# Attention scores contracted over 128 rows, and two memory regions placed alike by 512 bytes

## What is computed

```python
mod = silu(c) @ ada_w.T + ada_b            # shifts, scales, gates
h   = modulate(rmsnorm(x), scale_msa, shift_msa)
q, k, v = split(h @ qkv_w.T + qkv_b)       # 16 heads of 36
q, k = rmsnorm(q) * 36 ** -0.5, rmsnorm(k)
o   = softmax(q @ k.T) @ v
x   = x + tanh(gate_msa) * (o @ proj_w.T + proj_b)
h2  = modulate(rmsnorm(x), scale_mlp, shift_mlp)
x   = x + tanh(gate_mlp) * (gelu(h2 @ fc1_w.T + fc1_b) @ fc2_w.T + fc2_b)
```

## Time and profile before

| what | us |
|---|---|
| median of 3 runs (lowest to highest) | 2906.13 (2906.03 to 2906.17) |
| the profiled execution | 2906.52 |
| its span in the trace | 2904.7 |
| first stage, to 436 us | 436 |
| attention, 436 to 1867 us | 1431 |
| PE busy in the span | 2880.2 (99%) |
| DVE / ACT / POOL busy | 1968.6 / 1578.1 / 213.3 |

### The profile page before, as it was taken

One profiled execution on the slowest core, in us unless ns is written; L12 is line 12 of the kernel. 1 busy time (PEld: TensorE's weight loads), 2 busy tenths in 40 slices (PEclk: granted clock), 3 DMA queues, 4 the chain that ended last, 5 costly groups with the idle time before them and its releaser, 6 DMA issues.

```text
span 2904.7 us, 35301 instructions
## 1 busy us (share of the span) xinstructions
PE 2880.2 (99%) x12990; PEld 2175.9 (75%) x12990; DVE 1968.6 (68%) x2727; ACT 1578.1 (54%) x1924; POOL 213.3 (7%) x161
## 2 busy tenths in 40 slices
PE   8999999999999999999999999999999999999999
PEld 7999986666666666666666666788888888888887
DVE  7777778899888888888888887844344243424342
ACT  4334336776776677677677666634344343434342
POOL 1323310101000000000000000090000000000000
PEclk9999999999999999999999999999999999999999
DMA  6555554221322322222222223432222222322121
GB/s 229 164 190 171 176 172 131 87 77 59 88 74 77 85 76 63 81 80 78 76 80 68 74 84 92 137 122 86 74 86 74 82 78 87 98 90 87 41 69 50
DMA packets 238454, 282.67 MB, mean 97 GB/s; under 512 B 34960, under 2 KB 144016, under 8 KB 237392
## 3 DMA queue, kind: packets, MB, share of 16 engines
q1 hardware_dynamic: 233408, 270.80, 30.4%
q10 hardware_dynamic: 4880, 9.70, 1.0%
HBM read 195.50 MB, written 84.67 MB: 96 GB/s over the span
## 4 chain that ended last, share of the span: by engine, by line
PE 94%; DVE 3%; ACT 1%; DMA 1%; issue 0%; SPq 0%; POOL 0%; POOLq 0%; DVEq 0%; ACTq 0%
PE ps L1645 16%; PE ps L1670 16%; PE ps L1733 15%; PE ps L1715 15%; PE ps L1657 13%; PE ps L794 12%; PE ps L1691 4%; PE ps L1656 2%; PE ps L749 1%; ACT gated L1314 1%; DMA gain<-kg 0%; DVE p_lo L1457 0%; DVE x L1517 0%; PE ps L741 0%; DVE w_lo L1510 0%
## 5 line engine op out<-in xcount | busy, mean ns | idle before, releaser
L1258 ACT ACTIVATE p_r<-ps 128x1024 f32<-128x1024 f32 x512 | 491.8, 1025 | 406.4 <-PE ps L1645 406.4
L1457 DVE TENSOR_TENSOR p_lo<-p_r,p_hi 128x1024 fp32r<-128x1024 f32 x512 | 613.7, 1220 | 0.0
L1645 PE MATMUL ps<-qT,kT 110*128 110x512 f32 x2048 | 574.7, 398 | 2.8 <-DMA kT<-qk_hi_scratch 1.7
L1645 PEld LDWEIGHTS ps<-qT,kT 110*128 110x128 f32 x2048 | 382.8, 190 | 137.7 <-issue 51.4
L1258 ACT ACTIVATE prob<-ps 128x1024 f32<-128x1024 f32 x512 | 483.5, 1031 | 3.1 <-PE ps L1645 2.8
L1656 PE MATMUL ps<-prob,vp 128*64 128x512 f32 x1024 | 453.1, 595 | 0.0
L1657 PE MATMUL ps<-prob,vp 128*37 128x512 f32 x1024 | 451.7, 594 | 0.0
L1587 DVE TENSOR_TENSOR a_lo<-act,a_hi 128x512 fp32r<-128x512 f32 x144 | 101.6, 706 | 508.2 <-ACT a_hi L1301 508.2
L1451 DVE CAST p_hi<-p_r 128x1024 fp32r<-128x1024 f32 x512 | 350.5, 695 | 135.7 <-ACT p_r L1258 134.2
L1733 PE MATMUL ps<-a_hi,w 128*128 128x512 f32 x1296 | 415.4, 393 | 0.0
L1670 PE MATMUL ps<-p_hi,vx 128*128 128x512 f32 x1024 | 404.3, 395 | 0.1
(11 more groups left out here) (194 smaller groups left out, 3556.0 us busy)
## 6 DMA issues: line engine op xcount, KB each, us to landing
w_raw<-w SPq DMA_DIRECT2D x144, 320.0 KB, 2.9
qk_hi_scratch<-aw SPq DMA_DIRECT2D x32, 576.0 KB, 3.2
qk_lo_scratch<-aw SPq DMA_DIRECT2D x32, 576.0 KB, 4.4
kT<-qk_hi_scratch SPq DMA_DIRECT2D x128, 144.0 KB
qT<-qk_hi_scratch SPq DMA_DIRECT2D x128, 144.0 KB
v_scratch<-stv SPq DMA_DIRECT2D x32, 512.0 KB, 2.7
vp<-v_scratch SPq DMA_DIRECT2D x16, 1024.0 KB, 9.2
xb<-xT SPq DMA_DIRECT2D x8, 1280.0 KB, 10.9
```

Of the source, the lines that this page charges most:

```text
L1258: act.activation(out, ps[:, 2 * slot:2 * slot + 2, :].rearrange("p a b -> p (a b)"), ACT.Exp).then_inc(exp_done, 1)
L1457: dve.tensor_tensor(p_lo[:, j], p_r[:, j], f32(p_hi[:, q % HIGHS]), ALU.subtract).then_inc(plo_done, 1)
L1645: mm = pe.matmul(ps[:, 2 * (entry % RING) + h, :], kT[r][:, h, kt * P:(kt + 1) * P], qT[:, u % 2, h], start=True, stop=True)
```

## The change

Three things are edited.

- `kT0`, `kT1` and `qT` get 128 partitions in place of 110, so each score matmul contracts 128 rows. The memsets of ones reach to row 127. Rows 96 to 127 of `qT` are set to zero by two new POOL memsets, one for each of its two buffers, after the first and the second memset of `kT0`; the loads of q then overwrite rows 96 to 109. So rows 110 to 127 add ones times zeros.
- A semaphore `qzero` counts these two. SP waits for one of them before it loads the first q, and for both before the second.
- `W2` is lowered to the next place that has the low region's remainder by 512 bytes: from byte 146368 to 146176 (280 times 512 above 2816). `WP` and `OB` follow it. All tiles that PE reads in the second and third stage then have the same remainder, 256, but for the columns of `vp` named above.

```diff
@@ FirstUnit
-        self.kT = nc.alloc_sbuf_tensor_at("kT0", [PKW, 2, N], F32R, offset=base)
+        self.kT = nc.alloc_sbuf_tensor_at("kT0", [P, 2, N], F32R, offset=base)
...
-        self.qT = nc.alloc_sbuf_tensor_at("qT", [PKW, 2, 2, BLK], F32R, offset=base + 8 * N + 4 * NT * VP)
+        self.qT = nc.alloc_sbuf_tensor_at("qT", [P, 2, 2, BLK], F32R, offset=base + 8 * N + 4 * NT * VP)
...
+        self.qzero = sem("qzero")
@@ qkv_phase, SP, last tile group
                         sp.wait_ge(first_unit.kones, 1)
+                        sp.wait_ge(first_unit.qzero, 1)
@@ qkv_phase, POOL
-            pool.memset(f32(first_unit.kT[96:PKW, :, c * BLK:(c + 1) * BLK]), 1.0).then_inc(first_unit.kones, 1)
+            pool.memset(f32(first_unit.kT[96:P, :, c * BLK:(c + 1) * BLK]), 1.0).then_inc(first_unit.kones, 1)
+            if c < 2:
+                pool.memset(f32(first_unit.qT[96:P, c]), 0.0).then_inc(first_unit.qzero, 1)
@@ main_phase
-    W2 = top - 8 * FC * D
+    W2 = low_end + (top - 8 * FC * D - low_end) // 512 * 512
...
-    kT[1] = following("kT1", [PKW, 2, N], F32R)
+    kT[1] = following("kT1", [P, 2, N], F32R)
@@ load_q
+                if u == 1:
+                    sp.wait_ge(first_unit.qzero, 2)
@@ POOL
-            pool.memset(f32(kT[1][96:PKW]), 1.0).then_inc(kones, 1)
+            pool.memset(f32(kT[1][96:P]), 1.0).then_inc(kones, 1)
```

## The result

The changed kernel takes 2886.61 us (median of 6 runs, 2885.45 to 2887.21) against 2906.35 for the one before (6 runs, 2906.03 to 2907.42): a ratio of 0.9931, 95% interval 0.9921 to 0.9942. The profiled execution took 2886.55 us, its span 2884.8. That is 19.7 us less; 21 were forecast.

The account below looks back on a forecast made before the run. PE was taken to bound the kernel, hardly waiting, with unsettled matmul distances to gain from. Attention 13.1 plus MLP 7.9, rows and memsets nothing, made 21.0 us off, to 2885.2 us; range 2880 to 2899, forecast case 0.64.

Parts of the forecast that it names:

- The floor: Settled distance from one 512-element matmul's start to the next, 0.2266 us, read from the projection and split values after the last unit.
- Attention: Scores and split values, 64 matmuls a unit, 64 units: 16.0 us less 1.9 for settling and 1.0 for five units, 13.1.
- The excess of 0.25 us a unit: In attention, 64 matmuls take 14.95 us against 14.50 at 0.2266 each; 0.20 of the 0.45 stays with the form switches.
- The five units beside POOL: Attention units where POOL splits projection weights and DVE casts run long; PE would wait longer, 5 x 0.2 = 1.0 us off.
- MLP: fc1 and fc2: a step's 28 matmuls fall from 6.40 to 6.345 us, 0.055 a step, 144 steps, 7.9 us gained.
- The row count: Score matmuls contracting 128 rows instead of 110: no extra time taken, bounds nothing to 11.9 us more.
- The third witness: First stage, L794: slices 1728 bytes apart, so remainders differ all the time; its mean of 361 ns stands 4 above 357.
- Memsets and waits: New POOL memsets and SP's wait before loading q: 33 us of cover, so cost nothing, bound 1 us.
- Half of it: Rival: remainder or neighbour explains only one stage, so only the MLP gains (2898) or only attention (2893); chance 0.20.
- Slower: Rival: in the scores the 128-row contraction costs 11.9 us and the remainder brings nothing, 2918; chance 0.06.
- Nothing: Rival: matmul distances come from the order of lines and banks, addresses are irrelevant, time stays 2906; chance 0.10.
- One sign that failed: Among the signs of a right forecast: durations of value matmuls, ACT and DVE stay unchanged.

## Why the prediction was right, and where its reasons weren't

- **The floor.** 0.2266 us a matmul was the right floor. Nearly all matmuls of 512 elements outside the switches came to it, and no kernel held a shorter distance.
- **Attention, 13.1 forecast, 13.3 measured.** The excess of 0.25 us a unit was right: 14.95 became 14.72, with 0.02 to 0.03 kept, as the 0.03 taken from the projection's rows after the last unit. The agreement of the sum is closer than that of its parts. 64 times 0.23 would be over 14. The five units beside POOL lost less of the gain than I took, 0.6 us together and not 1.0, and the last three distances from unit to unit, which I left out, lost 0.4: from the first value matmul at 1777.37 to that at 1856.11 before, and from 1764.52 to 1843.01 after, only 0.25 was gained and not 0.68. Part of the 0.2 us of agreement is therefore luck. For the five units, in the changed kernel the same place reads:

```profile
529.01 2.79 DVE L1457 CAST p_hi<-p_r 128x1024 fp32r<-128x1024 f32 x2 [2.06 <-ACT p_r L1264]
...
533.65 1.52 PE L1651 MATMUL ps<-qT,kT 128*128 128x512 f32 x6
535.41 0.47 PE L1676 MATMUL ps<-p_hi,vx 128*128 128x512 f32 x1 [0.24 <-issue]
```

  The casts of DVE are as long as in the earlier trace rows; six scores to the split value take 1.76 instead of 1.65, so the start of the split value comes 0.11 later behind its scores, and not the 0.2 that I took off.
- **MLP, 7.9 forecast, 6.8 measured.** The term was oversized in three ways. The typical step fell from 6.400 to 6.347, by 0.053 and not 0.055, which makes 7.6 for 144. And PE's waits at the block boundaries grew: those for DVE before fc1 from 2.0 us in the page of before to 2.6, which fits DVE's and ACT's work between two blocks not having shortened with PE's. And the layout has an exception that I overlooked when I wrote that all tiles PE reads come to one remainder: `ones`, the stationary operand of two sums of squares (L1709 and L1710) in seven of the steps, lies among the small tiles at byte 1664, with remainder 128 by 512 in both kernels. Such a step in the changed kernel:

```profile
2209.60 0.39 PE L1721 MATMUL ps<-mh_hi,w_hi 128*128 128x512 f32 x1
...
2213.26 0.63 PE L1739 MATMUL ps<-a_hi,w 128*128 128x512 f32 x2
...
2215.34 0.61 PE L1739 MATMUL ps<-a_hi,w 128*128 128x512 f32 x2
...
2216.48 0.39 PE L1721 MATMUL ps<-mh_hi,w_hi 128*128 128x512 f32 x1
```

  Nine fc2 matmuls right behind the two sums take 2.08 (2213.26 to 2215.34), 0.231 each, and the step 6.88, as it did before (2224.95 to 2231.83): these seven gained nothing, some 0.4 us. The steps with a projection chunk gained a little more than the others, as I had left out. Whether placing `ones` alike would win the 0.4 back wasn't tried.
- **The row count, cost nothing: right in the changed kernel, wrong as a reason.** I took the row count to be nothing and leaned on the remainder. The run with the rows alone and that with the placing alone showed that rows are half of the matter: with equal remainders, 110 or 127 rows beside 128 give a unit of 22.05, which is slower than before. So this step of the reasoning was wrong, and the forecast came out right in spite of it. The sum came out because I had costed both edits together from a stretch in which both were equal. Had the change only been the placing, the same reading would have forecast some 20 us, and about 2 would have come.
- **The third witness was false.** L794 does stand above its floor, but its slices' places are the smaller part of it: equal places gave 1.2 us where 6 were expected, and only with streams of 512 elements, at equal places, did it settle.
- **The Trainium skill's rules.** "TensorE: Matmul & The Clock Gate", section "Step-by-step: what each phase is for", says that the moving operand and the weight load have read ports of their own, so that loading the next weights doesn't steal from the running matmul, and that the row count doesn't matter to the load. The first doesn't hold as a rule of time in the runs here: moving `vx` alone by 64 bytes costs 0.33 us a unit. The second is about the load alone, and the runs don't contradict it: 128 rows in place of 110, with the placing left, kept the unit at 21.95. What costs is a change of the row count from matmul to matmul, 0.31 us a unit for a single row. All this is 1 to 2% of a unit.
- **Memsets and waits, nothing: right.** The new memsets ran from 379.67 and 396.33 us for about 1 us each, and SP's first load of k started at 414.07.
- **The rivals.** "Half of it" was what the placing alone does in the MLP, minus what it costs in attention. "Slower" had the right object (row counts matter) and the wrong sign: it is 128 beside 110 that costs, not 128. "Nothing" is out: one line of placing took 0.05 us off each step.
- **One sign that failed.** ACT's durations were to stay as they were, and the scores' exponentials got longer records; the last section has them. It cost nothing here.

## What to carry to other kernels

When PE is busy 99% and waits for nothing, measure the distance from start to start of equal matmuls in several places; if one line has two values, there is something to gain without removing work. Here fp32r matmuls ran at 0.2267 us when three things came together: the same number of contracted rows from one to the next, moving and stationary operands at the same remainder (by 512 bytes; in attention by 256 was enough), and streams of 512 elements. Where one was missing, such a stretch took about 1 to 3% more. Try such conditions together before judging them apart, since one alone may show nothing or a loss.

## What the runs showed of the hardware that I had not expected

- Row counts of 127 and 110 beside 128 cost the same, 0.31 us in a unit of 32 scores and 32 split values.
- The cost of unequal places has no single order. At 0, 64, 128 and 192 bytes apart an MLP step took 6.35, 6.47, 6.43 and 6.40 us, most at 64; an attention unit with 128 rows throughout took 21.74, 21.84, 21.93 and 21.95, most at 192. Why the distances cycle (0.226, 0.229, 0.232 before; 0.236, 0.231 at 64 apart) isn't known; that two streams from memory get in each other's way fits, but was only argued.
- ACT's records of the scores' exponentials became longer in the changed kernel, in the mean 1067 and 1056 ns instead of 1025 and 1031 (L1264, before L1258), but their work didn't. The records overlap, and six of them between the same points of a unit take 5.42 us from start to start (1014.63 to 1020.05) against 5.50 before (1019.52 to 1025.02); the busy time of the first group went only from 491.8 to 494.2 us. Over all kernels here the mean of that group goes with the unit's length: 1025 to 1026 ns where the unit takes 21.96 or more, 1034 at 21.93 and 21.95, 1044 at 21.84, 1066 to 1068 at 21.74 and 21.75. Why wasn't tested.

```profile
L1264 ACT ACTIVATE p_r<-ps 128x1024 f32<-128x1024 f32 x512 | 494.2, 1067 | 397.5 <-PE ps L1651 397.5
...
1014.63 5.62 ACT L1264 ACTIVATE prob<-ps 128x1024 f32<-128x1024 f32 x6
1020.05 3.84 ACT L1264 ACTIVATE p_r<-ps 128x1024 f32<-128x1024 f32 x4
```
